# Cross-attention on one core: norm scaling moved to the first key slot, output weights split in halves between the key blocks, first batch's score steps moved from token slots to key slots

## The reference

```python
def _L0_xattn_ref(x, latents, attention_mask, ...):   # x: (16,256,512) context, latents: (16,256,512)
    h = jnp.concatenate([x, latents], axis=1)
    q = (latents @ q_w + q_b).reshape(b, k_len, NH, DH)
    kv = (h @ kv_w + kv_b).reshape(b, p + k_len, NH, DH, 2)
    kmat, v = (kv[..., 0], kv[..., 1])
    attn = jnp.einsum('bkhd,bnhd->bhkn', q, kmat) / DH
    attn = jnp.where(full_mask[:, None, None, :], attn, -jnp.inf)
    attn = jax.nn.softmax(attn.astype(jnp.float32), axis=-1)
    attn_out = jnp.einsum('bhkn,bnhd->bkhd', attn, v).reshape(b, k_len, H)
    attn_out = attn_out @ out_w + out_b + residual
    out = rmsnorm(attn_out, postnorm_w)
    out = jax.nn.gelu(out @ mlp_w1 + mlp_b1) @ mlp_w2 + mlp_b2
    return out + residual
```

## Time and profile before

| | |
|---|---|
| time, median of 3 runs | 2487.04 us (2487.03 to 2487.82) |
| the profiled execution: time, span | 2487.28 us, 2485.5 us |
| busy PE / DVE / ACT / POOL | 95% / 50% / 58% / 9% |
| mean granted TensorE clock | 0.98 of 2.4 GHz |

### The profile page before, as it was taken

The page is one execution under the profiler, slowest core; times in us unless marked ns, Lnnn a source line. Parts: engine busy times, 40 slices in busy tenths (PEclk is TensorE's granted clock), DMA queues, the critical chain, the costliest instruction groups (busy, mean ns, idle before and its releaser), DMA issues. The chain is left out here.

```text
span 2485.5 us, 43834 instructions
## 1 busy us (share of the span) xinstructions
PE 2362.6 (95%) x14656; PEld 1918.6 (77%) x14656; DVE 1243.4 (50%) x2447; ACT 1430.1 (58%) x3322; POOL 226.2 (9%) x260
## 2 busy tenths in 40 slices
PE   6999999999999999989999999999889999999998
PEld 5777777777777777668888888888777878787776
DVE  4455566666666666552122112212367676767674
ACT  3777777777777777743222222222256767676666
POOL 1000000000000000010000000000211111111210
PEclk9899999999999999889999999999889999999998
DMA  6344444444444443532011011102245454545443
GB/s 183 79 108 109 107 108 109 107 107 108 107 106 107 107 107 92 140 122 73 5 51 51 0 51 51 47 4 84 69 109 147 113 143 114 142 115 140 117 122 86
DMA packets 148187, 239.01 MB, mean 96 GB/s; under 512 B 25600, under 2 KB 59680, under 8 KB 148144
## 3 DMA queue, kind: packets, MB, share of 16 engines
q1 hardware_dynamic: 139024, 225.48, 33.4%
q10 hardware_dynamic: 9120, 12.98, 2.3%
HBM read 86.28 MB, written 25.21 MB: 45 GB/s over the span
## 5 line engine op out<-in xcount | busy, mean ns | idle before, releaser
L571 ACT ACTIVATE l_score_ps<-l_score_ps,l_neg_max 128x512 f32<-128x512 f32 (+1 forms) x1024 | 566.4, 557 | 273.3 <-DVE l_neg_max L818 273.1
L818 DVE TENSOR_REDUCE l_neg_max<-l_score_ps 128x1 f32<-128x512 f32 (+1 forms) x768 | 494.9, 683 | 51.5 <-PE l_score_ps L1112 49.4
L591 ACT ACTIVATE l_probs<-l_score_ps 128x1024 f32<-128x1024 f32 x384 | 382.4, 1018 | 80.6 <-PE l_score_ps L1145 78.8
L1477 ACT ACTIVATE mlp_hidden<-mlp_hidden_ps,mlp_b_col 128x512 f32<-128x512 f32 x128 | 88.3, 690 | 496.2 <-PE mlp_hidden_ps L67 496.0
L1112 PE MATMUL l_score_ps<-l_stack 97*128 97x512 f32 (+1 forms) x1024 | 314.9, 372 | 47.7 <-ACT l_score_ps L571 35.3
L1512 DVE TENSOR_TENSOR mlp_hidden_l<-mlp_hidden,mlp_hidden_h 128x512 fp32r<-128x512 f32 x128 | 94.6, 739 | 517.3 <-ACT mlp_hidden_h L1479 517.2
L1145 PEld LDWEIGHTS l_score_ps<-l_stack 99*128 99x128 f32 x1536 | 213.7, 193 | 59.5 <-ACT l_score_ps L571 18.4
L1145 PE MATMUL l_score_ps<-l_stack 99*128 99x256 f32 x1536 | 245.2, 292 | 15.0 <-ACT l_score_ps L571 13.9
L1112 PEld LDWEIGHTS l_score_ps<-l_stack 97*128 97x128 f32 x1024 | 175.1, 193 | 100.5 <-ACT l_score_ps L571 74.0
L571 ACT ACTIVATION_READ_ACCUMULATOR l_score_ps<-l_score_ps,l_neg_max 128x1 f32 x1024 | 212.6, 208 | 0.0
L65 PE MATMUL mlp_hidden_ps<-mlp_norm_h,mlp_w_l 128*128 128x512 f32 x512 | 200.3, 391 | 6.4 <-DVE mlp_norm_l L1507 6.4
(11 more groups left out here) (139 smaller groups left out, 4211.2 us busy)
## 6 DMA issues: line engine op xcount, KB each, us to landing
l_stack<-room SPq DMA_DIRECT2D x248, 192.0 KB
l_stack<-l_qk SPq DMA_DIRECT2D x192, 128.0 KB
l_stack<-room SPq DMA_DIRECT2D x124, 128.0 KB
l_stack<-l_qk SPq DMA_DIRECT2D x222, 64.0 KB
l_tokens<-in_x SPq DMA_DIRECT2D x16, 512.0 KB, 3.4
l_tokens<-in_ctx SPq DMA_DIRECT2D x16, 512.0 KB, 4.2
l_rows<-in_x SPq DMA_DIRECT2D x16, 512.0 KB, 3.4
norm_transposed<-norm_room SPq DMA_DIRECT2D x16, 512.0 KB, 2.7
```

The lines of the kernel that those rows point to most:

```text
L571: m = act.activation(e, e, ACT.Exp, bias=neg_max[:, q, h:h + 1], accum_out=row_sum[:, q, h:h + 1])
L591: act.activation(probs[:, s % PROBS, :].rearrange("p (a b) -> p a b", a=2), score_ps[:, 2 * (s % 2):2 * (s % 2) + 2, :], ACT.Exp).then_inc ...
L818: dve.tensor_reduce(out, bank, AXIS_X, ALU.max, negate=True).then_inc(max_done, 1)
L1477: act.activation(hidden[:, m % HBUF, :], hidden_ps[m % 4][:, :], ACT.Gelu_apprx_tanh, bias=b1_col[:, m:m + 1])
```

## The change

Four edits, all of layer 0.

```diff
-    STEPS_AT_FIRST = [0, 0, 4, 4, 4, 4, 4, 4, 4, 4] if first else [0, 0, 2, 3, 3, 3, 3, 2]
-    STEPS_IN_SLOT = [2, 4, 4, 2, 1, 2, 1, 4, 4, 4] if first else [2, 1, 2, 1, 2, 3, 3, 2]
+    STEPS_AT_FIRST = [0, 0, 0, 2, 2, 2, 2, 8, 8, 8] if first else [0, 0, 2, 3, 3, 3, 3, 2]
+    STEPS_IN_SLOT = [2, 4, 4, 2, 2, 2, 1, 4, 4, 3] if first else [2, 1, 2, 1, 2, 3, 3, 2]
...
-    SQUARE_SLOT, SCALE_SLOT, NORM_SLOT = 1, 3, TURN_SLOT + 1
+    SQUARE_SLOT, SCALE_SLOT, NORM_SLOT = 1, TURN_SLOT, TURN_SLOT + 1
...
             for u, w, scale in ((3, wq, SCALE), (2, wo, 1.0)):
                 src = stage[u % 2].rearrange("p (f n) -> p f n", f=FB)
-                split_ops.append((u, src, [t[:, :, :] for t in w], scale))
+                for c in range(2):
+                    part = slice(2 * c, 2 * c + 2)
+                    split_ops.append((u, src[:, part, :], [t[:, part, :] for t in w], scale))
...
-            SPLITS_OF_K, SPLITS_OF_Q, SPLITS_OF_V = 2, 5, 5
-            FIRST = (T_ITEMS + [("split", n) for n in range(4)] + K_ITEMS[:2] + [("split", 4)] + K_ITEMS[2:] + Q_ITEMS
-                     + [("split", 5)])
+            SPLITS_OF_K, SPLITS_OF_V, SPLITS_OF_Q = 2, 4, 6
+            FIRST = (T_ITEMS + [("split", n) for n in range(4)] + K_ITEMS[:2] + [("split", 4)] + K_ITEMS[2:3]
+                     + [("split", 5)] + K_ITEMS[3:] + [("split", 6), ("split", 7)] + Q_ITEMS)
...
+        def turn_slot(a):
+
+            return TURN_SLOT + 1 if first and isinstance(a, int) and a == 0 else TURN_SLOT
...
-                        if first and prev is not None and slot == NORM_SLOT + 1 and k < steps[-1]:
+                        if first and prev is not None and slot == NORM_SLOT + 1 and k < steps[1] + HALVES:
```

More of the change, by code:

```diff
@@ L127, in attention_layer @@
     TURN_SLOT = AFTER_T
-    SQUARE_SLOT, SCALE_SLOT, NORM_SLOT = 1, 3, TURN_SLOT + 1
-    assert max(STEPS_IN_SLOT + STEPS_AT_FIRST) <= RING
+    SQUARE_SLOT, SCALE_SLOT, NORM_SLOT = 1, TURN_SLOT, TURN_SLOT + 1
+    assert max(STEPS_IN_SLOT + STEPS_AT_FIRST[:AFTER_T]) <= RING
     assert len(STEPS_IN_SLOT) == SLOTS and AHEAD + sum(STEPS_IN_SLOT) == STEPS
@@ L676, in iteration @@
                     if a is not None:
-                        if TURN_SLOT == slot - 1:
+                        if turn_slot(a) == slot - 1:
                             copy_shift(a, 0)
@@ L914, in iteration @@
                             step_max(a, k)
-                    if a is not None and TURN_SLOT == slot:
+                    if a is not None and turn_slot(a) == slot:
                         make_shift(a, 0)
```

## The result

| | before | after |
|---|---|---|
| time, median of 5 runs each | 2487.04 us (2486.46 to 2488.41) | 2476.14 us (2473.19 to 2478.13) |
| ratio | | 0.9953, interval 0.9939 to 0.9968 |
| profiled execution: time, span | 2487.28, 2485.5 us | 2477.08, 2475.3 us |
| end of batch 0's round (first row of the output projection's last step on DVE) | 123.81 | 108.04 |
| mean of the 14 rounds behind it | 63.228 | 63.515 |

The change is faster by 10.9 us, where 26.3 were forecast; the time is 2 us above the range. Up to the end of layer 0 the gain is 11.2 us: batch 0 brings 15.8 (forecast 16.4), and the 14 rounds, which should have become 9.1 shorter, become 14 x 0.287 = 4.0 longer; the last batch becomes 0.55 longer.

A forecast was written before the change was run, and what follows sets the result against it. PE was taken to set the pace in a round's first pass, losing a little at hand-overs. Batch 0's 16.4, the rounds' 9.1 and the last batch's 0.8 sum to 26.3 off 2487.04, giving 2460.7 us; range 2452 to 2474.

The forecast's parts named there:

- batch 0: First batch's pass with new step table and split order: 93.19 becomes 76.4, 16.8 less; 16.4 us taken as gain.
- the last batch: Batch without token items: scaling moved and slot 9 shorter, between 0 and 1.3 us less; 0.8 taken.
- What is next late: Rounds: norm tile's store makes ACT's copy wait 0.3 us, hidden; SP's other loads move with PE and ACT events.
- 14 x 0.65 = 9.1: Rounds of batches 1 to 14: step and scaling moves gain 0.68 us each, taken as 0.65; 9.1 us in all.
- the lateness of slot 8: Rounds' first pass: slot 8 runs 0.7 us late for PE, ACT and DVE; slot 9's shorter row makes it up.
- Rival 2: Rounds: PE's lateness of slot 8 is not made up, each 0.45 us longer, 2476.1 us; chance 0.10.
- hand-over: Engine-to-engine times read off the trace, such as exponential to exponential 0.66 us and exponential to PE's bank reuse 0.83.
- PE's waits for sums in the token slots: Rounds after the step move: PE's scores wait for ACT, losing 0.73, 0.43, 0.12 and 0.42 us.
- The scaling: Moved from slot 3 to 7: PE's low-part wait until 392.33 goes; costs DVE 0.79 us, 0.2 of it showing.
- The store of the norm tile: Rounds: issued at 408.46, lands 2.7 us later at 411.16; ACT's copy waits 0.3 us, hidden with a microsecond left.
- Rival 4: Norm tile's store lands late and holds ACT's copy, each round 1.6 us longer; time 2492 us; chance 0.04.
- Rival 1: Clock falls in batch 0's key slots; two of three at half clock give 6 us back, 2466.7 us; chance 0.20.

The follow-up runs named there:

- Experiment 1: Changed kernel plus one wait: POOL's bias addition to the rows waits until PE has turned the shift tile of half 1; 2460.42 us, ratio 0.9893.
- Experiment 6: Kernel before with one score step moved from slot 9 to 4 and POOL's bias addition held until half 1's shift is turned; 2475.95 us, ratio 0.9952.
- experiments 8 and 9: Kernel before with batch 0's step table and later shift alone (8): 2481.04 us; with batch 0's split order alone (9): 2482.08 us.
- experiment 4: Kernel before with batch 0's edits alone (step table, later shift, split order), rounds' table and scaling unchanged; 2470.37 us, ratio 0.9932.
- experiment 10: Changed kernel with POOL's bias addition in four pieces of 256 columns instead of two of 512, no new wait; 2474.59 us, ratio 0.995.
- experiment 5: Kernel before with the rounds' step move alone (one score step from slot 9 to slot 4); 2491.35 us, ratio 1.0015.
- experiment 3: Kernel before with POOL's bias addition lengthened from 2.5 to 5 us by two more pieces on the first row tile; 2537.12 us, ratio 1.0202.
- experiment 11: Changed kernel with POOL's addition held until half 1's shift is turned, and one more step moved from slot 8 to 6; 2476.98 us, ratio 0.9961.

## Why the prediction was wrong

**The step that failed** is "What is next late" in the part on the rounds, and with it the term of 14 x 0.65 = 9.1. It asked which other work the lateness of slot 8 and the earlier end of slot 9 touch, and went through PE, ACT, DVE and SP, but not POOL. The term measured -4.0, 13.1 us off. POOL was busy 3.8 of 35.5 us in the first pass and nobody waits for it there, so I had treated its place as free. Experiment 1 gives the term as 14 x 0.741 = 10.4 when POOL is away. What failed was an overlap: the prediction had PE reach `turn_shift` with the tile there (409.17), and PE stood 1.01 us for it, because DVE's cast took 1.28 us beside POOL instead of 0.17.

**A number that came out by chance.** Rival 2, PE's lateness of slot 8 not made up, gave 2476.1, and 2476.14 was measured. Its mechanism did not happen: `shifted(1)` came 0.51 us earlier and without a wait. Its rounds were to be 0.45 longer each and are 0.29 longer, for another reason, and batch 0, the last batch and what lies behind layer 0 make up the difference.

**Of the chain itself** every hand-over held. Last exponential: 0.75 earlier, forecast 0.70. `shifted(1)`: 0.51 earlier and without a wait, forecast 0.42. `turn_shift` with POOL away: 0.75 earlier, forecast 0.68. PE's waits for sums in the token slots came to 0.9 us where I had added up 1.7.

**The scaling** was credited with the wait that goes from the token slots. Experiment 6 against 1 shows that its place doesn't matter once the step has moved: rounds of 62.487 in both. Without the scaling's move PE waits 0.24 us for ACT and 0.47 for a low part of DVE in the token slots, with it 0.52, 0.17 and 0.19, all for ACT.

**The store of the norm tile** was hidden, as forecast: it was issued at 393.70 and takes 2.7 us, and ACT's copy follows at 397.11 directly behind an exponential, so the forecast wait of 0.3 us is not there after. In experiment 1, where the pass ends as early as forecast, it is: the store is issued at 388.19, and the copy starts at 390.95 after an idle time of 0.27 (which the profile puts down to PE; the 2.7 us of the store end at the same moment). Rival 4 named a true kind of trouble, a transfer that becomes late through slot 8, but looked at the store and not at the load of the rows beside it.

**Batch 0**: right in all (-15.8 for -16.4, with 1.1 us lost to the same cast; -17.1 with POOL away), but in part by luck. The terms written out for ACT add up to 57.1 + 23 x 0.66 + 1.4 + 2.4 = 76.1 for the start of the last exponential, not to the 75.2 that the sum goes on with. Measured is 56.70 + 15.2 + 1.4 + 1.8 = 75.10: the time lost at the slots' begins and at the shift was put 0.6 too high, the start 0.4, and a slip of 0.9 made up for both. Its division between the parts was not in the prediction's sum and was wrong when I made it (experiments 8 and 9).

**The clock.** Rival 1 was that the clock falls in batch 0's key slots. It did not: 1.00 from 45.80 to 76.50, while PE cycled through four PSUM banks with waits of 0.16 to 0.75 us. By the rule of the Trainium skill on such cycling ("TensorE: Matmul & The Clock Gate", section "A second HAM failure mode: psum-queue depth-cycling") the clock would have swung; this trace does not agree. But a fall is not far off: in experiment 4, with the same order in batch 0, there is one stretch of 3.4 us at 0.50 from 68.2 on, behind waits of 0.63, 0.18 and 0.17 us, and its round ends 1.1 us later than after's. After has the same three waits (0.63, 0.16 and 0.17) and no fall; what decides between the two, no run shows. In the rounds the waits of the earlier trace rows are 0.27 to 0.69, not up to 0.9 as the prediction has it.

**The last batch**: -0.8 was forecast and +0.55 measured; with POOL away it is -0.65. Neither can be laid to the change: the same code for this batch takes 56.39 us in before and 54.44 in experiment 4, with the clock at 0.50 for 17.1 us of it in the one and 13.7 in the other.

**Account.** With POOL away, up to the end of layer 0: 17.1 + 10.4 + 0.65 = 28.2 us, 27.7 between the spans of the two profiled executions, and 26.0 in the medians (2486.39 beside it against 2460.42). The forecast of 26.3 was that of a kernel in which the meeting doesn't take place. The change as it stands gave 10.9.

## What to carry to other kernels

An engine that is nearly idle and that nobody waits for can still set the pace, if one of its instructions holds what another engine's short instruction needs: when work moves, follow every engine's instructions through the stretch in which the critical chain ends, and ask how far apart the two that may not meet are (here at most 0.23 us, in 15 of 16 batches). A maximum far above the median in the view of a tile (632 ns against 170) can be such a meeting in the making, and worth a look before a sum is made. When one arises, hold the idle engine's work back behind the chain, if nobody needs it there; here cutting it into pieces only moved the stall to the next instructions.

## What the runs showed of the hardware

- DVE casts of 128x16, SBUF to SBUF, take 0.17 us alone and up to 1.31 beside a POOL addition of 128x512 (1.28 us a piece). The long ones end 0.03 to 0.04 us behind the end of a piece, in every run. POOL's pieces keep their 1.26 to 1.30 us.
- A DVE subtraction of 128x16 with both inputs in SBUF: 0.17 alone, 0.77 beside a piece of 0.72 (experiment 10). A reciprocal of 128x16, SBUF to SBUF, keeps its 0.24 us beside POOL (155.42 in experiment 5), and so do maxima and weighings that read PSUM.
- The clock can fall in the rounds as well: in experiment 3 in 10 of 14 rounds, inside PE's wait of some 2 us for the shift tile or up to 1.5 us behind it; in experiment 11 in 5 of 14, near the end of the last of three waits of 0.53, 0.17 and 0.66 (which lie within 2.4 us) or up to 0.7 us behind it. Other rounds of both kernels have the same waits and no fall. 3.4 us at 0.50 cost 1.1 us a round in experiment 11 and 1.4 in experiment 3. In experiment 1, with 0.9 us of waits in a round (0.52, 0.17, 0.19), no round has such a stretch.
- POOL's time per piece of this addition: 1.28 us for 512 columns, 0.73 for 256.
